# The tenth table of a DLRM tower gathered by GpSimd instead of looked up by one-hot products

## The reference, cut to what matters

```python
e = jnp.stack([tbl_0[ids[:, 0]], ..., tbl_25[ids[:, 25]]], axis=1)     # (2048, 26, 128)
v = jnp.concatenate([dense[:, None, :], e], axis=1)                    # 27 vectors
flat = jnp.einsum('bnd,bmd->bnm', v, v)[:, rows, cols]                 # 351 pairs
h = jnp.concatenate([dense, flat, dense], axis=1)
h = jnp.maximum(h @ W_top1 + b_top1, 0.0)                              # 607 -> 512
h = jnp.maximum(h @ W_top2 + b_top2, 0.0)                              # 512 -> 256
y = h @ W_top3                                                         # 256 -> 1
```

## Time and profile before

| | us |
|---|---|
| median of 3 executions (lowest, highest) | 372.37 (372.17, 372.56) |
| the profiled execution, its own time | 371.39 |
| its span, first to last instruction | 369.6 |
| TensorE matmuls busy | 334.6 (91%) |
| TensorE weight loads busy | 310.2 (84%) |
| VectorE busy | 244.6 (66%) |
| ScalarE busy | 138.8 (38%) |
| GpSimd busy | 245.9 (67%) |
| TensorE's mean granted clock | 0.99 of 2.4 GHz |

### The profile page before, as it was taken

The page is one execution under the profiler, slowest core; times in us unless marked ns, Lnnn a source line. Parts: engine busy times, 40 slices in busy tenths (PEclk is TensorE's granted clock), DMA queues, the critical chain, the costliest instruction groups (busy, mean ns, idle before and its releaser), DMA issues.

```text
span 369.6 us, 14433 instructions
## 1 busy us (share of the span) xinstructions
PE 334.6 (91%) x6192; PEld 310.2 (84%) x6192; DVE 244.6 (66%) x702; ACT 138.8 (38%) x232; POOL 245.9 (67%) x260
## 2 busy tenths in 40 slices
PE   0766789999899899999999999999999999998986
PEld 0665789989798898989899898989899898997775
DVE  4999998989465684659667694659667694611110
ACT  2246332536043250435334260435324260435322
POOL 5877777777777777777777777777777777720000
PEclk9998999999999899999999999999999999999999
DMA  6999943242244211531244211532244211300000
GB/s 192 276 265 245 284 134 124 57 126 52 59 150 124 59 50 50 156 121 52 55 116 153 58 50 50 156 121 50 57 132 138 57 50 50 85 21 4 18 2 0
DMA packets 16758, 36.94 MB, mean 100 GB/s; under 512 B 5661, under 2 KB 8733, under 8 KB 16735
## 3 DMA queue, kind: packets, MB, share of 16 engines
q1 hardware_dynamic: 8479, 19.80, 17.9%
q0 software_dynamic: 8192, 16.79, 17.3%
q10 hardware_dynamic: 64, 0.01, 0.0%
HBM read 36.57 MB, written 0.01 MB: 99 GB/s over the span
## 4 chain that ended last, share of the span: by engine, by line
PE 84%; DVE 6%; DMA 3%; issue 3%; SPq 2%; ACT 1%
PE gram L418 14%; PE hid L384 13%; PE look_odd L338 8%; PE look_odd L340 8%; PE look_ps L338 7%; PE look_ps L340 7%; PE vec_act L311 7%; PE hid L392 7%; DVE onehot L572 4%; PE hid L338 4%; PE hid L340 4%; DMA raw<-tbl 3%; DVE look_lo L580 2%; PE small L353 1%; SPq L245 1%
## 5 line engine op out<-in xcount | busy, mean ns | idle before, releaser
L292 POOL DMA_INDIRECT vecs<-tbl,ids_sb x256 | 245.7, 960 | 80.0 <-issue 77.5
L572 DVE TENSOR_SCALAR onehot<-step_ids,row_no 125x256 fp32r<-125x256 int32 x640 | 202.4, 387 | 43.1 <-PE look_odd L340 23.0
L547 ACT COPY vecs_T<-vec_act 128x512 f32<-128x512 f32 x64 | 46.0, 731 | 78.2 <-PE vec_act L311 78.2
L338 PE MATMUL look_odd<-onehot,look_hi 125*128 125x256 f32 x256 | 69.6, 306 | 5.4 <-DVE look_lo L580 5.4
L338 PE MATMUL look_ps<-onehot,look_hi 125*128 125x256 f32 x256 | 67.2, 299 | 4.7 <-DVE look_lo L580 2.9
L340 PE MATMUL look_odd<-onehot,look_lo 125*128 125x256 f32 x256 | 63.9, 284 | 0.0
L340 PE MATMUL look_ps<-onehot,look_lo 125*128 125x256 f32 x256 | 63.8, 285 | 0.0
L418 PE MATMUL gram<-vecs_T 128*27 128x26 f32 x4096 | 52.3, 193 | 9.6 <-issue 5.3
L418 PEld LDWEIGHTS gram<-vecs_T 128*27 128x27 f32 x4096 | 43.7, 104 | 18.9 <-issue 15.7
L338 PEld LDWEIGHTS look_odd<-onehot,look_hi 125*128 125x128 f32 x256 | 49.0, 191 | 7.3 <-DVE look_lo L580 6.2
L338 PEld LDWEIGHTS look_ps<-onehot,look_hi 125*128 125x128 f32 x256 | 49.4, 193 | 5.6 <-DVE look_lo L580 5.3
(11 more groups left out here) (70 smaller groups left out, 275.7 us busy)
## 6 DMA issues: line engine op xcount, KB each, us to landing
step_ids<-look_ids SPq DMA_DIRECT2D x15, 640.0 KB
raw<-tbl SPq DMA_DIRECT2D x10, 448.0 KB
vecs<-tbl,ids_sb POOLq DMA_INDIRECT x256
dense_new<-dense SPq DMA_DIRECT2D x8, 128.0 KB
dense_T<-dense SPq DMA_DIRECT2D x8, 128.0 KB, 2.3
raw<-tbl SPq DMA_DIRECT2D x10, 52.0 KB
step_ids<-look_ids SPq DMA_DIRECT2D x1, 512.0 KB
w_sb<-w SPq DMA_DIRECT2D x1, 512.0 KB
```

Source lines behind the costliest of these rows:

```text
L292: nc.gpsimd.indirect_dma_start(out=vecs[j][:, k, :], out_offset=None, in_=tables[k], in_offset=bass.IndirectOffsetOnAxis(ap=ids_sb[:, t, k ...
L338: nc.tensor.matmul(bank, look_hi[:, f, ch, :], onehot[:, i % SLOTS, c, :], start=ch == 0, stop=False)
L547: return engine_copy(vecs_T[j][:, :, lo:lo + GROUP], bank[:, :, :].rearrange("d v b -> d b v"))
L572: last = nc.vector.tensor_scalar(onehot[:, i % SLOTS, c, :], step_ids[a][0:LOOK_K, f - a * LOOKUPS // 2, :], row_no[0:LOOK_K, ch:ch + 1], ...
```

## The change

From pair 2 on, table ten is no longer looked up. GpSimd gathers its rows, behind the gathers of the pair's even tile: two indirect DMAs, one for each tile of the pair, into a new buffer `last_rows`. For pairs 3 to 7 the first of the two waits until the units and transposes of the pair before are done (`onehot_used`). TensorE turns the two blocks of rows by two transposes into the second half of the bank that the lookups wrote before, and adds the two counts to `onehot_used` that units 8 and 9 gave. VectorE's unit 7 of an odd tile adds three to `onehot_made`. The odd tile's order changes too: group 3 is turned directly behind group 2, then come unit 6, the products, layer 3, unit 7, and the two transposes; ScalarE's `relu2` moves ahead of its unit 7. Sync loads ids for four tables instead of five in the odd step. Behind the loop, half of layer 1 is ahead of the last tile's groups, and half of layer 2 and the fold's transposes lie between its two halves; the products of the last tile stand together.

```diff
+ROWS_FROM = 2
...
-                    load_step(2 * r + 1, 1, r)
+                    load_step(2 * r + 1, 1, r, slice(0, STEP_IDS - 1))
...
+                def gather_last(pair):
+
+                    if pair > ROWS_FROM:
+                        pool.wait_ge(onehot_used, 2 * LOOKUPS * pair)
+                    for j in range(2):
+                        nc.gpsimd.indirect_dma_start(
+                            out=last_rows[:, j, :], out_offset=None, in_=look_tables[LOOKUPS - 1],
+                            in_offset=bass.IndirectOffsetOnAxis(ap=ids_sb[:, 2 * pair + j, GATHERS:GATHERS + 1], axis=0),
+                        ).then_inc(last_rows_in, 16)
...
                 for t in range(1, tiles):
                     gather(t)
+                    if t % 2 == 0 and t // 2 >= ROWS_FROM:
+                        gather_last(t // 2)
...
+                def turn_last(pair):
+
+                    pe.wait_ge(last_rows_in, 2 * 16 * (pair - ROWS_FROM + 1))
+                    for j in range(2):
+                        lo = PAIR + j * P
+                        last = nc.tensor.transpose(look_ps[DUO_BANK[DUOS - 1]][:, lo:lo + P], last_rows[:, j, :], ident[:, :])
+                    last.then_inc(onehot_used, 2)
...
                     turn_group(n, k, 2)
+                    if mlp and j == 1:
+                        turn_group(n, k, 3)
+                        unit(6)
+                        gram_first(t, j, pair)
+                        gram_second(j)
+                        layer3(pair - 1)
+                        unit(7)
+                        turn_last(pair + 1)
+                        return
...
                 gram_second(0)
+                layer1(pairs - 2, 1)
                 turn_half(last, 1, pairs - 1, 0)
+                layer2(pairs - 2, 0)
+                pairs_out(last - 1, 1, pairs - 1, bank=pairs_end)
                 turn_half(last, 1, pairs - 1, 1)
-                layer1(pairs - 2, 1)
                 gram_first(last, 1, pairs - 1)
-                pairs_out(last - 1, 1, pairs - 1, bank=pairs_end)
-                layer2(pairs - 2, 0)
                 gram_second(1)
-                    if mlp and j == 1:
-                        layer3(pair - 1)
...
+                    full = LOOKUPS - 2 if rows else LOOKUPS
...
-                            make_unit(t + 2, j, *made[i])
+                            make_unit(t + 2, j, *made[i], 1 + LOOKUPS - full if i == full - 1 else 1)
...
-                    for i in range(TURN_UNIT, LOOKUPS):
+                    for i in range(TURN_UNIT, full):
                         unit(i)
```

More of the change, by code:

```diff
@@ L107, in sem @@
             return ctx.enter_context(nc.semaphore(name))
-        ids_sb = sb("ids_sb", [P, tiles, GATHERS], I32)
+        ids_sb = sb("ids_sb", [P, tiles, GATHERS + 1], I32)
+        last_rows = sb("last_rows", [P, 2, D])
         vecs = [sb(f"vecs{j}", [P, ROWS, D]) for j in range(2)]
@@ L174, in build @@
         gathered = [[sem(f"gathered{j}_{h}") for h in range(2)] for j in range(2)]
-        first_ids_in = sem("first_ids_in")
+        first_ids_in, last_rows_in = sem("first_ids_in"), sem("last_rows_in")
         step_ids_in = [sem(f"step_ids_in{a}") for a in range(2)]
@@ L564, in turn, with make_unit @@
                                               gram_rows[:, 0, :, 1:HALF]).then_inc(folded, 1)
-                def make_unit(s, a, i, f, half):
+                def make_unit(s, a, i, f, half, count=1):
                     if positive(LOOKUPS * s + i + 1 - SLOTS):
@@ L574, in make_unit @@
                             row_no[0:LOOK_K, ch:ch + 1], None, ALU.is_equal)
-                    last.then_inc(onehot_made, 1)
+                    last.then_inc(onehot_made, count)
                 def take_low(f):
@@ L581, in take_low, with tile @@
                                             ALU.subtract).then_inc(table_split, 1)
-                def tile(t, j, pair, first=False, look=True):
+                def tile(t, j, pair, first=False, look=True, rows=False):
                     made = units(j)
+                    full = LOOKUPS - 2 if rows else LOOKUPS
                     def unit(i):
                         if look:
-                            make_unit(t + 2, j, *made[i])
+                            make_unit(t + 2, j, *made[i], 1 + LOOKUPS - full if i == full - 1 else 1)
                     if look:
@@ L623, in _ @@
                     tile(2 * r, 0, r)
-                    tile(2 * r + 1, 1, r)
+                    tile(2 * r + 1, 1, r, rows=True)
                 last = tiles - 1
@@ L733, in tile @@
                         merge(1, pair, False)
+                    if mlp and j == 1:
+                        relu2(pair - 1)
                     unit(7)
@@ L736, in tile @@
                         relu1(pair - 1, 0)
-                    if mlp and j == 1:
-                        relu2(pair - 1)
                     unit(9)
@@ L778, in _ @@
                 relu1(pairs - 2, 0)
-                for q in range(GROUPS):
+                relu1(pairs - 2, 1)
+                for q in range(HALF_GROUPS):
                     copy(last, 1, q)
-                relu1(pairs - 2, 1)
                 copy_pairs(last - 1, 0, pairs_end)
+                for q in range(HALF_GROUPS, GROUPS):
+                    copy(last, 1, q)
                 relu2(pairs - 2)
@@ L810 @@
         "dense": dense,
-        "ids": np.ascontiguousarray(ids[:, large].reshape(-1, P, GATHERS).transpose(1, 0, 2)),
+        "ids": np.ascontiguousarray(ids[:, large + small[-1:]].reshape(-1, P, GATHERS + 1).transpose(1, 0, 2)),
         "look_ids": np.ascontiguousarray(ids[:, small].T.reshape(2, LOOKUPS // 2, -1, 2 * P).transpose(0, 2, 1, 3)
```

## The result

The changed kernel takes 381.31 us (median of 4 executions, 378.96 to 382.47) against 372.27 for the kernel before beside it (4 executions): ratio 1.0252, 95% interval 1.021 to 1.0295. Three of the four executions of before are those of the table ahead. It is slower, 9.0 us on the medians, where 2.8 were forecast; 381.31 lies outside the range given. The profiled execution took 380.31 us and its span is 378.5, 8.9 us over that of before.

What follows compares the result with a forecast made beforehand. TensorE was taken to bound the loop, with GpSimd just 3% faster. The terms 2.05 - 1.69 + 1.6 + 0.4 + 0.4 gave +2.8 us, from 372.37 to 375.2 us; range 372.2 to 378.0.

Steps and rivals of the forecast that it cites:

- The sign: Whole kernel: the change makes it slower, by 2.8 us; chance of slower 0.82.
- It waits 2.1 us: Even tiles of rounds 2 to 6: TensorE waits 2.1 us for VectorE's fold, five times, 10.5 us; bounds 1.8 and 2.4.
- The rest of a round: Rounds 2 to 6: 1.69 us saved on TensorE against 2.1 us of waiting, +0.41 us a round.
- Rival 4: Loop: wait of 2.4 us (+1.5) and even tiles' products as dear as odd ones' (+1.6); 378.3 us, chance 0.12.
- GpSimd's floor: Loop's end: ten more gathers, 12.6 us, keep group 2 of tile 13 from starting before 299.8; not felt.
- rival 2: Loop: fold wait under 1.8 us, so TensorE waits for gathered rows and GpSimd bounds; 373.7 us, chance 0.18.
- Tile 13's products, "+1.6": Last odd tile: its products now run among gathers and cost 1.6 us more; bounds 0 and 1.9.
- The first half of tile 14's products, "+0.4": Behind the loop: this half, 1.39 us before without gathers, costs 0.4 us more.
- The reordered end … +0.4: Behind the loop: products wait 1.2 us for ScalarE's last copy, 0.4 us more in all; bounds -0.8 and +1.2.
- The last round, "-1.69": Last round: dropping units 8 and 9 for two transposes saves TensorE 1.69 us.
- Rival 3: Every tile's products: gaps come from the code's place and the shifted code loses them; 371.2 us, chance 0.08.

Runs made afterwards that it cites:

- the four that wait for rows: Changed kernel with two units ahead of the turn (375.67 us), that plus the earlier end order (371.69), fold's transposes later (375.6), or products last plus earlier end order (373.48).
- the old end: Changed kernel with the order of the kernel before behind the loop, on TensorE and ScalarE: 379.98 us, ratio 1.020 to the kernel before.

## Why the prediction was wrong

The sign was right, and so were the wait and its place; what a wait costs, and what the new end costs, were not.

- **"It waits 2.1 us" for the fold, five times.** Right: 1.84 us once and 1.95 to 1.99 four times, in the place and for the reason given. The step that failed is what was made of it: 10.5 us of waiting, priced as nothing but time. TensorE, 98% busy in a round of before, had no such idleness there to show what its clock does behind it. Three low stretches at 1.36 us are 4.1 us. With the 2.2 of the next point, less the 1.45 named there, they are about the 4.6 missing up to group 2 of tile 13. Filling the wait shows it by ratio: 4.6 us back, with 1.9 us of useless work in each wait. The bounds of 1.8 and 2.4 were those of the wait alone.
- **The rest of a round.** An undisturbed round is 42.60 against 41.63, +0.97 where +0.41 was forecast. Layer 3 takes 0.63 instead of 0.36 us, the transposes of gathered rows 3.26 instead of 3.02, and the two tiles' products 7.44 instead of 7.23 together: the even tiles pay 0.4 to 0.6 more, the odd ones 0.4 less. Rival 4 had the even tiles' part of that. Layer 3's part is not its own: it is 0.36 or some 0.6 us in the kernel before with the new end too, and the odd tile's products are then 3.80 or 3.63, and without gathers it is 0.36 in every round. A hole of the gathers falls into the one or the other; products and layer 3 of an odd tile are 4.05 together, 4.16 before. From layer 2 of round 2 to that of round 6 the forecast was missed by 4 x 0.56 = 2.2 us here and by 4.1 by the clock; with the forecast's 1.64 this is the 7.99 us that these four rounds grew by. The round before them gives 1.45 back against the forecast: there the kernel before has a low stretch of its own, at 123, and takes 44.91 us. That is luck of the trace: the mean clocks of other executions of that kernel run from 0.986 to 1.0, so that they have other numbers of low stretches.
- **GpSimd's floor.** Right, and never felt in the changed kernel, which comes too late for it. It is what the versions without the wait for the fold ran into, as rival 2 said: group 2 of tile 13 at 298.5 to 299.9 in the four that wait for rows, for a floor of 299.8. The last gather starts at 338.57 (forecast 340.3).
- **Tile 13's products, "+1.6".** 3.31 us to the next instruction instead of 2.18, +1.1, and +0.25 on layer 3 behind them. Its cause is shown by the gathers added to the kernel before (3.70 there) and by those taken from it (2.2 in every tile).
- **The first half of tile 14's products, "+0.4".** Nothing: 1.40 us against 1.39 before, since it began at 340.32, when the last gather was over.
- **"The reordered end … +0.4".** The second step that failed. The wait for the last copy was seen: the 16 transposes with their waits rose from 2.53 to 2.85 us, +0.3. That the products then stand in one piece was told of in the change and priced at nothing; they take 4.87 instead of 1.20 and 1.75: +1.9. The bound of +1.2 had doubled the wait and left the products out. The hole of 1.33 us up to 122.11 in the kernel before, shown above, was a row for such a price. The one of 1.08 us at 333.54 is not: it stands ahead of a piece and not in it, with 1.08 us in all traces but one, and no packet goes with it.
- **The last round, "-1.69".** Right: the two units' products and the new transposes together -1.8.
- **Rival 3** (the gaps are the code's) is false for the loop, by the kernel without gathers, and holds for the end. I had put one cause to all gaps; there are two.

The end then sums to -1.8 + 1.1 + 0.25 + 1.9 + 0.3 = +1.75, and 48.24 - 46.42 is 1.82.

What stays open: why the low clock follows three waits of five and not the other two of nearly the same length; and what in a gather makes the holes of the loop.

## What to carry to other kernels

A wait on an engine that has been nearly always busy costs more than its length: price it with the time at the lower clock behind it, from any row of the kernel at that level, here 2.0 us of waiting plus 1.36 in three cases of five. When one engine's work is moved to another, look at what the freed engine's order now waits for; here one line, units made ahead of the turn, was worth some 6 us, and still the gathers' pitch left nothing of a saving of 10. And count short instructions in one piece as a cost where code runs once.

## What was not expected of the hardware

- The clock. Behind waits of 1.84 to 2.36 us in the loop it fell to the lower level nine times in thirteen: three of five in the changed kernel, three of four with the old end, and behind waits of 2.27, 1.84 and 2.36 us in others, but not behind one of 2.29. Behind waits of 0.7 to 1.3 us in the loop it did not. Holes count as well: a low stretch goes with four of the six holes of 2.1 to 2.75 us in the last products, and with that of 1.33 us up to 122.11 in the kernel before. The Trainium skill's "TensorE: Matmul & The Clock Gate", section "What's actually happening", has low as the default that activity lifts; the filled wait agrees.
- With the gathers, 256 records of TensorE's short products take 3.4 to 4.0 us instead of 2.2, and a round 2.8 us more, without sharing data with them. What is shared is not shown.
- A hole of 2.2 to 2.95 us in straight code with 256 product records in a row, at a place that moves with the code.
